# A dilation whose relus are moved into PSUM, where TensorE adds onto them

## The reference, cut to what matters

```python
def dilation(u, kernel, r):               # r = 5, ks = 11, NEG = -1e30
    pad = jnp.pad(u, ((0, 0), (0, 0), (r, r), (r, r)), constant_values=NEG)
    def body(acc, idx):
        di, dj = idx // ks, idx % ks
        sl = jax.lax.dynamic_slice(pad, (0, 0, di, dj), (Bn, C, H, W))
        return jnp.maximum(acc, sl - kflat[:, idx][None, :, None, None]), None
    ...                                   # over all 121 taps
...
x = x + _L0_conv_ref(_gn(x), L0_conv_finsler_params)   # the dilation
x = x + _L1_conv_ref(_gn(x), ...)                      # not touched here
```

## Time and profile before

| | before |
|---|---|
| median of three runs | 11728.51 us |
| span of the profiled execution | 11726.8 us |
| dilation stage, about 200 to 9766 us | 64 chunks |
| DVE busy, whole span | 11256.4 us (96%) |
| PE busy | 10455.5 us (89%) |
| POOL busy | 10018.7 us (85%) |
| ACT busy | 9189.6 us (78%) |
| an add onto `t` by DMA, issue to landing | 8.4 us (640 of them) |

### The profile page before, as it was taken

How to read it: one execution, slowest core, us unless ns; L and a number is a source line. 1 busy time by engine, 2 the same in 40 slices (tenths; PEclk the granted TensorE clock), 3 DMA queues, 4 the chain that set the end, 5 groups by cost and what they waited for, 6 DMA issues and landing times. The chain is left out here.

```text
span 11726.8 us, 92131 instructions
## 1 busy us (share of the span) xinstructions
PE 10455.5 (89%) x23180; PEld 4353.8 (37%) x23180; DVE 11256.4 (96%) x7096; ACT 9189.6 (78%) x5145; POOL 10018.7 (85%) x3019
## 2 busy tenths in 40 slices
PE   2999999999999999999999999999999997886665
PEld 1333333333333333333333333333333333332222
DVE  8999999999999999999999999999999998998999
ACT  2888888888888888888888888888888886776666
POOL 2999999999999999999999999999999996666777
PEclk9999999999999999999999999999999998998888
DMA  7555555555555555555555555555555553343555
GB/s 280 105 108 105 107 104 106 106 105 100 105 103 105 103 104 103 106 108 108 105 107 108 106 106 106 106 108 105 106 105 107 106 103 128 151 167 157 213 214 213
DMA packets 352237, 1435.57 MB, mean 122 GB/s; under 512 B 18896, under 2 KB 125520, under 8 KB 289616
## 3 DMA queue, kind: packets, MB, share of 16 engines
q0 software_dynamic: 183440, 762.23, 35.9%
q1 hardware_dynamic: 168256, 667.25, 15.3%
HBM read 465.90 MB, written 201.33 MB: 57 GB/s over the span
## 5 line engine op out<-in xcount | busy, mean ns | idle before, releaser
L502 POOL TENSOR_TENSOR m_pool<-r_pool,u 128x2048 f32<-128x2048 f32 x1792 | 7708.4, 4369 | 864.9 <-DVE acc_a L675 556.3
L531 PE MATMUL m_pe<-u,mats 128*128 128x512 f32 x10240 | 5375.2, 606 | 508.0 <-DVE acc_b L657 398.9
L533 PE MATMUL m_pe<-r_pe,mats 128*128 128x512 f32 x10240 | 5273.8, 596 | 0.0
L675 DVE SCALAR_TENSOR_TENSOR acc_a<-m_pool,kt,acc_a 128x2048 f32<-128x2048 f32 x1728 | 4059.9, 2349 | 54.5 <-POOL m_pool L502 41.0
L657 DVE SCALAR_TENSOR_TENSOR acc_b<-m_pe,kt,acc_b 128x1024 f32<-128x1024 f32 x2560 | 3246.0, 1278 | 103.2 <-PE m_pe L533 100.5
L531 PEld LDWEIGHTS m_pe<-u,mats 128*128 128x128 f32 x10240 | 1837.4, 191 | 3285.4 <-issue 1856.8
L533 PEld LDWEIGHTS m_pe<-r_pe,mats 128*128 128x128 f32 x10240 | 1948.4, 190 | 2510.3 <-issue 2510.3
L675 DVE SCALAR_TENSOR_TENSOR acc_a<-u,kt,acc_a 128x2048 f32<-128x2048 f32 x896 | 2103.8, 2348 | 4.5
L621 ACT ACTIVATE r_pool<-dx,gap_l 128x2048 f32<-128x2048 f32 x896 | 1778.6, 1993 | 329.7 <-POOL m_pool L502 326.2
L621 ACT ACTIVATE r_pe<-dx,gap_l 128x2048 f32<-128x2048 f32 x832 | 1659.1, 1994 | 364.2 <-PE m_pe L533 349.9
L592 ACT ACTIVATE t<-dx,gap_r 128x2048 f32<-128x2048 f32 x640 | 1284.7, 2007 | 10.4
(11 more groups left out here) (139 smaller groups left out, 5595.1 us busy)
## 6 DMA issues: line engine op xcount, KB each, us to landing
t<-dx POOLq DMA_DIRECT2D x640, 1059.0 KB, 8.4
u<-x_dram SPq DMA_DIRECT2D x28, 3328.0 KB, 28.7
xw<-x_scratch SPq DMA_DIRECT2D x64, 1152.0 KB, 6.9
hw<-h_scratch SPq DMA_DIRECT2D x66, 1024.0 KB, 8.9
x<-xc POOLq DMA_DIRECT2D x65, 1024.0 KB, 8.0
xt<-x_dram SPq DMA_DIRECT2D x32, 2048.0 KB, 14.4
xc<-x_dram SPq DMA_DIRECT2D x64, 1024.0 KB, 4.7
x_scratch<-x SPq DMA_DIRECT2D x64, 1024.0 KB, 9.6
```

Source lines behind the costliest of these rows:

```text
L502: nc.gpsimd.tensor_tensor(m_pool[slot(s, k, j, NPOOL)][:], r_pool[slot(s, k, j, NPOOL)][:], u[s][:, k * CR + di:k * CR + di + CR, base:bas ...
L531: nc.tensor.matmul(dst, ident, u[s][:, top:top + 2, base:base + W], start=True, stop=False)
L533: last = nc.tensor.matmul(dst, ident, r_pe[slot(s, k, j, NPE)][:, row:row + 2, :], start=False, stop=True)
L675: nc.vector.scalar_tensor_tensor(out=acc_a[:], in0=src, scalar=kt[:, col(di, base):col(di, base) + 1], in1=acc_a[:], op0=ALU.subtract, op1 ...
```

## The change

The relus that PE adds onto are now written straight into PSUM by ACT, and PE adds one term onto them with one identity matmul, without reading the relu from SBUF. The result stays in PSUM, so the next inner tap's relu can be taken of it in place. For six row sides (the left sides of rows 0 to 2, the right sides of rows 3 to 5) all taps of the side are folded that way, in a chain of four or five steps: relu, add `dx` (with the negated identity on a left side), relu, add `dx`, and so on; the last step adds `u`. There are two chains in work at a time, one for each half of the chunk (4 rows, 1024 elements). Only the end of a chain is merged by DVE.

Twelve pairs of a chunk go by DMA: ACT writes the relu into `t`, a DMA adds `u` onto it, and DVE merges `t` itself. POOL adds 24 pairs. The triples are gone. `r_pool` keeps two buffers, `m_pool` and `t` have three. The planner is replaced by four strings, one for each engine, in which each letter is an item: `0` and `1` a step or a merge of the chain of that half, `r` a relu for POOL, `x` a relu into `t`, `t` POOL's add, `i` an issue of the add by DMA, `m`, `y`, `s` DVE's merges of `m_pool`, of `t` and of a single tap, `b` the start of `acc_b`, `u` a sum, `n` and `d` the work on the next window, `a` the add of x.

```diff
+CHAINS = ((0, "left"), (1, "left"), (2, "left"), (3, "right"), (4, "right"), (5, "right"))
+NPOOL, NDMA = 24, 12
+ACT_ORDER = "rxr0x10r10r10r1bx10u10r1r01r0nx10r1x01r0n1r0r1xn01x0r10rn0x1r01rx0r10r1r01x0r1x01ru01x01r01r01r01"
+POOL_ORDER = "tttaditittditittdtititdittitttdititttidittt"
...
-        m_pe = [ctx.enter_context(nc.psum_tensor(f"m_pe{s}", [P, CR // 2, W], F32)) for s in range(2)]
+        chain = [ctx.enter_context(nc.psum_tensor(f"chain{h}", [P, HR, W], F32)) for h in range(2)]
...
+                def add_step(c, s, k, h, i):
+                    ch, step, base = chain_steps[i]
+                    di, side = CHAINS[ch]
+                    pe.wait_ge(chain_relu[h], c * NSTEP + (i + 1))
+                    if i == last_step[ch]:
+                        weight, src, dj = ident, u[s], base
+                    elif side == "left":
+                        weight, src, dj = neg_ident[:], dx[s], base
+                    else:
+                        weight, src, dj = ident, dx[s], base - 1
+                    for r in range(0, HR, 2):
+                        top = k * CR + di + h * HR + r
+                        added = nc.tensor.matmul(chain[h][:, r:r + 2, :], weight, src[:, top:top + 2, dj:dj + W],
+                                                 start=False, stop=True, skip_group_check=True)
+                    added.then_inc(chain_added[h], 1)
...
+                def chain_step(c, s, k, h, i):
+                    ch, step, base = chain_steps[i]
+                    di, side = CHAINS[ch]
+                    right = side == "right"
+                    src, scale = chain[h][:], 1.0
+                    if step == 0:
...
+                        act.wait_ge(chain_taken[h], at(c, NCHAIN, ch))
+                    else:
+                        act.wait_ge(chain_added[h], c * NSTEP + i)
+                    gap = gap_r if right else gap_l
+                    nc.scalar.activation(chain[h][:], src, ACT.Relu, bias=gap[:, col(di, base):col(di, base) + 1],
+                                         scale=scale).then_inc(chain_relu[h], 1)
...
+                    elif kind == "y":
+                        dve.wait_ge(t_added[j % TP], c * (NDMA // TP * 16) + (j // TP + 1) * 16)
+                        passed(dve, dve_turns)
+                        di, base, outer = dma_pairs[j]
+                        src = t[j % TP][:, :, 0:W]
```

More of the change, by code:

```diff
@@ L63, in passed @@
     engine.sem_inc(turns, 1)
[L66 to L82, removed]
-        singles += [(di, base), (di, outer)]
[L86 to L114, removed]
@@ new lines, in dilation_taps @@
+def dilation_taps():
+    pairs, singles = [], []
+    for di in range(KS):
+        side = dict(CHAINS).get(di)
+        if side == "left":
+            pairs += [(di, 5, 6), (di, 7, 8), (di, 9, 10)]
+        elif side == "right":
+            pairs += [(di, 1, 0), (di, 3, 2)]
+            singles += [(di, 4)]
+        else:
+            pairs += [(di, 5, 4), (di, 3, 2), (di, 6, 7), (di, 1, 0), (di, 8, 9)]
+            singles += [(di, 10)]
+    while len(pairs) > NPOOL + NDMA:
+        di, base, outer = pairs.pop()
+        singles += [(di, base), (di, outer)]
+    return pairs[NDMA:], pairs[:NDMA], singles
@@ L352, in col @@
         return di * KS + dj
+    chain_steps = []
+    for ch, (di, side) in enumerate(CHAINS):
+        bases = range(1, 5) if side == "left" else range(9, 4, -1)
+        chain_steps += [(ch, step, base) for step, base in enumerate(bases)]
+    last_step = [max(i for i, x in enumerate(chain_steps) if x[0] == ch) for ch in range(len(CHAINS))]
+    NSTEP, NCHAIN = len(chain_steps), len(CHAINS)
+    NA = sum(kind in "mys" for kind in DVE_ORDER)
+    a_after = {}
+    for kind, j in numbered(DVE_ORDER):
+        if kind in "mys":
+            a_after[kind, j] = len(a_after) + 1
     with ExitStack() as ctx:
@@ L382, in dilation @@
         t_ready = sem("t_ready")
[L383 removed]
+        t_added = [sem(f"t_added{s}") for s in range(TP)]
         pool_turns = sem("pool_turns")
@@ L492, in _ @@
                             c = i * CH_IT + (s * CPW + k)
[L493 to L506, removed]
+                            for kind, j in numbered(POOL_ORDER):
+                                if kind == "t":
+                                    pair(c, s, k, j)
+                                elif kind == "i":
+                                    add_u(c, s, k, j)
+                                elif kind == "a":
@@ L521, in _ @@
                             c = i * CH_IT + (s * CPW + k)
[L522 to L535, removed]
+                            for half, j in numbered(PE_ORDER):
+                                add_step(c, s, k, int(half), j)
             @block.scalar
@@ L567, in _, with sum_before @@
-                act.sem_inc(r_pool_ready, NPOOL)
-                act.sem_inc(r_pe_ready, NPE)
+                def sum_before(c, which, shift_column):
+                    shift = shift1[:, bass.ds(shift_column, 1)]
+                    if which == 0:
+                        act.wait_ge(x_added, c * 16 + 16)
+                    else:
+                        act.wait_ge(x1_summed, c * 2 + 1)
+                    passed(act, act_turns)
+                    nc.scalar.activation(xc[:], x1[:], (ACT.Identity, ACT.Square)[which], bias=shift,
+                                         accum_out=sums1[:, which, bass.ds(c, 1)]).then_inc(x1_summed, 1)
@@ new lines, in pair_relu @@
+                def pair_relu(s, k, pair, dst):
+                    di, base, outer = pair
+                    right = outer > base
+                    lo = base if right else outer
+                    gap = gap_r if right else gap_l
+                    return nc.scalar.activation(dst, dx[s][:, k * CR + di:k * CR + di + CR, lo:lo + W], ACT.Relu,
+                                                bias=gap[:, col(di, base):col(di, base) + 1],
+                                                scale=1.0 if right else -1.0)
@@ L629, in _ @@
+                for which in range(2):
+                    sum_before(NCHUNK, which, NWIN)
             @block.vector
```

239 lines of the change are left out of this document (108 added, 131 removed).

## The result

The changed kernel takes 11150.2 us, the median of four runs (11148.28 to 11155.45), against 11726.87 before: a ratio of 0.951 (95% interval 0.9496 to 0.9523). That is 577 us less; 611 were forecast, and 11,115 us lies 35 us under the measured time.

The account below looks back on a forecast made before the run. The prediction took VectorE (DVE) to bound the kernel: 137.1 us of queue plus 2.4 of waits make 139.5 us a chunk for 149.05, 611 us less over 64 chunks, told as 11,115 us; 8-in-10 range 10,975 to 11,350.

Parts of the forecast that it names:

- DVE as the bound, and its price: VectorE's queue in the dilation: its instructions, priced by distances between starts, sum to 137.1 us a chunk; chance 0.66.
- The waits: VectorE's waits per chunk: 2.4 us, of which 1.4 at chains and buffers, 0.7 at DMAs, 0.3 at the join.
- ScalarE's sum: ScalarE's work per chunk: 68.4 us full relus, 55.1 half relus, 11 the rest; 134.5 us, bounds 129 and 139.5.
- The rival of ScalarE: ScalarE becomes the bound in the dilation: 143 us a chunk, 387 us less, 11,341 us; chance 0.18.
- Its signs: For ScalarE as bound: ACT busy over 97%, VectorE waiting 5 us a chunk for PE's chains and POOL's `m_pool`.
- The turn: Relu, TensorE's add, next relu in a chain: second half ready after 4.98 us, ScalarE's order reaches it at 4.96.
- The DMAs: Adds onto `t` landing late for VectorE's third merge behind window loads: 0.5 to 1 us a chunk, 0.7 taken.
- The clock: TensorE's granted clock in the dilation: 0.95 or more if the forecast holds, below 0.9 if its rival does.
- the rival: TensorE's clock falls in the dilation: at 0.83 a chunk takes 155.8 us, 432 us more, 12,160 us; chance 0.07.
- POOL: POOL's work per chunk: four adds fewer, two DMA issues more, busy 135.5 us falling to 121.5; no bound.

## Why the prediction was right

- **DVE as the bound, and its price.** 137.1 us of queue were forecast, 137.6 follow from the measured distances; 138.2 is what remains with ScalarE relieved, the difference being the waits around the join (0.4 and 0.2 us). Added merges cost their full price (7.6 us for 7.2), merges left out gave 1.0 us of it: DVE is not the only bound. The waits were forecast at 2.4 us a chunk, and 140.0 - 137.6 is 2.4 as well. That is luck in part: 1.4 at the chains and the buffers was 1.4 (32.2 and 7.6 us of 4000), but 0.7 at the DMAs was 0, which made up for 0.6 at the join, where 0.3 was forecast, and for gaps too short for the rows. With the waits equal, the 35 us between forecast and result are the 0.5 us by which the queue was priced too low.
- **ScalarE's sum.** 1.02 us for a half relu was 1.00, the sum 134.5 was 133.1. But the step that put it "2.6 us under DVE's 137.1" failed: it left the turns out of the sum. The loop with its turns is 139.0 us, level with DVE's 138.2. The kernel stands at two walls at once, and 140.0 is a little over both. The rival of ScalarE, with 0.18, had the loop nearly right ("134.5 and 5 of waits") and its price wrong: it put DVE's own waits on top and came to 143 us. Its signs did not show: ACT was 95% busy, and DVE waited 1.4 us a chunk for PE and POOL.
- **The turn.** That the turn "just about fits at full clock, without any reserve" was right: ACT waits 162 us of 4000 in its chains, and one matmul less per turn is worth 109 us.
- **The buffers.** The forecast nowhere names the third buffer of `m_pool`, and took the order of queues to work. It does, but only with it: 6.2 us a chunk. The sum over queues came out because this condition was met, and it had not been examined. That too is luck.
- **The DMAs.** 0.7 us a chunk were forecast for late landings; it is 0.1 at most (9 us in all). The third merge of `t` has little room, as forecast, 1.4 us at least. But the long landings are not those of the third add; they are those of the first two, and these have room.
- **The clock.** "0.95 or more" was 0.94. The argument against the rival held PE's longest idle times to be 2 to 3 us; they are up to 6.0. So the rival was real in its mechanism, and it has a share in the turns: most of ACT's waits for PE end at an add that ran at 1.2 GHz. Its price is small, since relieving ScalarE altogether is worth 1.8 us a chunk. How much of that is the clock's stays open, as no run holds the clock up.
- **POOL.** 121.3 us for 121.5, and it holds nobody up as long as it has its buffers.

## What to carry to other kernels

Sum each engine's queue by distances between starts, and for an engine that hands work back and forth add its turns to its sum before calling it slack: with two walls 1% apart a relief of one alone is soon stopped by the other (1.0 us of 7.2 here). Check what buffers the new order presumes; without one of them 394 of the 577 us were gone here. While GpSimd works on SBUF, let VectorE's merges read one of their two inputs from PSUM.

## What the runs showed of the hardware

- A VectorE merge with both tensor inputs in SBUF took 5.16 us in the mean, up to 16.03, beside POOL's adds, 2.45 us with these cut to an eighth, and 2.35 with one input in PSUM. The stall is inside the instruction's duration, and no group of waits shows it.
- A subtraction of a scalar by POOL (128 x 2048 f32) took 5.76 us, and the activation that does the same in the changed kernel 2.02:

```profile
L466 POOL TENSOR_SCALAR acc_b<-u,kt 128x2048 f32<-128x2048 f32 x28 | 161.2, 5756 | 0.0
```

```profile
L522 ACT ACTIVATE acc_b<-u,nkt x15: 2009/2016/2020, 3037.4 to 4995.8; 128x2048 f32<-128x2048 f32 x15
```

- With half the matmuls TensorE was still busy for 2384 of 4000 us, for 3102 in the changed kernel. A row took 2383.62 / 3125 = 0.76 us of busy time for 3102.41 / 6171 = 0.50, at a granted clock of 0.72 for 0.94: much of what was taken from TensorE's work came back in this way. How much of it is the clock, and how much that its rows stand in shorter groups, was not separated.
